# Hybrid block (Nystrom attention, FP4 feed-forward, linear attention): order of work where the first feed-forward meets linear attention

## The reference

```python
x = x + attn_a(layernorm(x), w_qkv, w_conv, w_fc, b_fc)
x = x + ffn(layernorm(x), w_gate, w_up, w_down)
x = x + attn_b(layernorm(x), W_attn, b_attn, W_proj, b_proj)
x = x + ffn(layernorm(x), w_gate, w_up, w_down)
```

```python
q, k = elu(q) + 1, elu(k) + 1          # the features
kv, ksum = kv + k_t v_t^T, ksum + k_t  # running sums over the tokens
y_t = (q_t kv) / (q_t . ksum + 1e-6)
out = y @ W_proj + b_proj
```

## Time and profile before

| | |
|---|---|
| median of 3 runs | 637.01 us (636.86 to 640.54) |
| the profiled execution | 637.31 us |
| its span, first to last instruction | 635.6 us |
| TensorE busy (matmul) | 577.8 us, 91% |
| VectorE busy | 487.4 us, 77% |
| ScalarE busy | 361.4 us, 57% |
| GpSimd busy | 303.3 us, 48% |
| mean granted clock of TensorE | 0.984 |

### The profile page before, as it was taken

How to read it: one execution, slowest core, us unless ns; L and a number is a source line. 1 busy time by engine, 2 the same in 40 slices (tenths; PEclk the granted TensorE clock), 3 DMA queues, 4 the chain that set the end, 5 groups by cost and what they waited for, 6 DMA issues and landing times.

```text
span 635.6 us, 14058 instructions
## 1 busy us (share of the span) xinstructions
PE 577.8 (91%) x5407; PEld 426.2 (67%) x5407; DVE 487.4 (77%) x1004; ACT 361.4 (57%) x679; POOL 303.3 (48%) x351
## 2 busy tenths in 40 slices
PE   4889998799999999987999988999999988599997
PEld 3777887466666679964777765656656655377776
DVE  6978888466666664887999876778778786889975
ACT  5643322344444443157998774556556557699975
POOL 6542111122223223546788677255554435667763
PEclk9999999799999999998999999999999999999999
DMA  9500000000000001000000000000000000000101
GB/s 248 135 2 1 3 2 2 1 1 1 2 1 2 1 3 35 2 0 1 1 2 2 1 1 1 3 2 2 2 2 2 1 3 2 1 18 18 34 18 51
DMA packets 15942, 9.58 MB, mean 15 GB/s; under 512 B 1478, under 2 KB 15750, under 8 KB 15876
## 3 DMA queue, kind: packets, MB, share of 16 engines
q1 hardware_dynamic: 15876, 8.69, 5.1%
HBM read 6.59 MB, written 2.10 MB: 14 GB/s over the span
## 4 chain that ended last, share of the span: by engine, by line
PE 43%; DVE 23%; POOL 14%; issue 11%; ACT 8%; DMA 1%; SPq 0%; POOLq 0%; DVEq 0%; ACTq 0%
PE ps L1440 6%; PE ps L1597 4%; PE ps L1456 4%; PE ps L1614 4%; PE ps L1635 3%; PE ps L1743 3%; PE ps L1619 3%; DVE r L965 3%; POOL G L335 3%; DVE m L1016 3%; PE ps L1447 3%; ACT S L549 2%; POOL arena L429 2%; ACT qbd L578 2%; PE ps L1630 2%
## 5 line engine op out<-in xcount | busy, mean ns | idle before, releaser
L394 POOL TENSOR_TENSOR A<-S,r 126x512 f32<-126x512 f32 x36 | 38.0, 1057 | 147.6 <-DVE r L968 132.9
L429 POOL TENSOR_SCALAR_AFFINE_SELECT arena<-arena 128x1024 f32<-128x1024 f32 x32 | 35.9, 1121 | 65.6 <-ACT arena L802 65.5
L1614 PE MATMUL ps<-wguT,xnt 128*128 128x352 f32 x128 | 52.1, 489 | 8.1 <-ACT xnt L642 5.4
L335 POOL TENSOR_TENSOR G<-S,hoff 128x704 f32<-128x704 f32 x31 | 47.1, 1520 | 24.9 <-DVE S L1112 24.7
L1635 PEld LDWEIGHTS ps<-wdT,xnt 128*128 128x128 f32 x372 | 48.5, 191 | 8.2 <-ACT xnt L649 1.4
L1635 PE MATMUL ps<-wdT,xnt 128*128 128x128 f32 x372 | 51.9, 275 | 0.9 <-ACT xnt L649 0.9
L802 ACT ACTIVATE arena<-ps 128x1024 f32<-128x1024 f32 x32 | 32.7, 1022 | 33.9 <-PE ps L1743 33.9
L1280 DVE TENSOR_TENSOR arena<-ps,XN 128x1024 f32<-128x1024 f32 x32 | 39.2, 1224 | 14.8 <-PE ps L1743 14.8
L965 DVE TENSOR_REDUCE r<-S 126x16 f32<-126x512 f32 x36 | 24.7, 685 | 33.4 <-ACT S L549 33.4
L1619 PE MATMUL ps<-wguT,xnt 128*128 128x352 f32 x128 | 44.2, 469 | 0.0
L549 ACT ACTIVATE S<-S 126x512 f32<-126x512 f32 x36 | 22.5, 625 | 38.1 <-DVE S L960 38.1
(11 more groups left out here) (225 smaller groups left out, 1520.2 us busy)
## 6 DMA issues: line engine op xcount, KB each, us to landing
X<-in_x SPq DMA_DIRECT2D x8, 256.0 KB, 5.5
out<-X SPq DMA_DIRECT2D x7, 256.0 KB, 2.3
arena<-in_wqkvT SPq DMA_DIRECT2D x4, 256.0 KB, 5.4
band<-in_band SPq DMA_DIRECT2D x1, 897.8 KB
arena<-in_wqkvT SPq DMA_DIRECT2D x1, 512.0 KB, 7.7
early<-in_wfc SPq DMA_DIRECT2D x1, 512.0 KB, 9.4
kI<-in_scaled_eye SPq DMA_DIRECT2D x1, 192.0 KB
XN<-in_wattn SPq DMA_DIRECT2D x1, 192.0 KB, 2.4
```

The lines of the kernel that those rows point to most:

```text
L335: tt(out=hgrid, in0=hmoved[k], in1=hoff[k][:, :], op=ALU.subtract).then_inc(s["fh_grid"], 1)
L394: tt(out=A1v[:, w % NW, :].rearrange("p (h m) -> p h m", m=M), in0=S1v[:, w % NW, :].rearrange("p (h m) -> p h m", m=M), in1=r1[:, 3, w % ...
L429: nc.gpsimd.affine_select(out=masked[n % 2][:, 8:16, :], in_=raw.rearrange("p (h t) -> p h t", t=P), pattern=[[0, 8], [1, P]], compare_op= ...
L1614: mm(ps[:, GATE_BANK, 0:F], xT[t // QD % 2][:, t % QD, :], wguT[:, 0:F], start=True, stop=True).then_inc(s["f_gate"], 1)
```

## The change

Seven edits in the hand-written orders:

- VectorE makes only h = 0 and 1 of the first quad's diagonals; ScalarE makes h = 3 and 2 in step r = 17 of the feed-forward, behind `lin_spread(0)` and `lin_xbT(1)` and ahead of `hT_copy(15)`. TensorE's wait in `lin_scores` counts ScalarE's two for every quad.
- TensorE issues `lin_k_mm(1)` directly behind `lin_scores(0)`, ahead of the last `down_mms`. ScalarE issues `lin_exp_k(1)` behind `lin_raw(0)`, ahead of the last `down_copy`.
- VectorE issues `lin_phi(1)` ahead of `lin_mask(1)`.
- GpSimd issues `lin_select(1)` and `lin_qk(1)` ahead of `layernorm_moments(2, 7)` and `lin_bias(1)`.
- VectorE issues `lin_v(0)` ahead of the statistics of step r = 16.
- ScalarE issues `down_copy(13)` between the two instructions of `offset_h(15)`.

```diff
--- before.py
+++ after.py
@@ -450,8 +450,6 @@
             lin_cap(1, eq, "lin_eq_done", "lin_eq_capped")
             lin_select(0)
             lin_cap(1, ek, "lin_ek_done", "lin_ek_capped")
-            layernorm_moments(2, QN - 1)
-            lin_bias(1)
             for n in range(TILES):
                 q, phase = (n + 1) // QD + 1, (n + 1) % QD
                 if n + 1 < TILES:
@@ -462,6 +460,9 @@
                         lin_cap(q, ek, "lin_ek_done", "lin_ek_capped")
                     if phase == 1:
                         lin_qk(q)
+                    if n == 0:
+                        layernorm_moments(2, QN - 1)
+                        lin_bias(1)
                     if phase == 2 and q + 1 < TILES // QD:
                         lin_bias(q + 1)
                 if n % QD == 1 and n > QD:
@@ -667,6 +668,8 @@
                     a.wait_ge(s["fh_ratio"], n + 1)
                     need(a, "fh_grid", n - 1)
                     act(hoff[r % 2][:, :].rearrange("p (k n) -> p k n", k=2), up_banks(r), ACT.Square, scale=SQ).then_inc(s["fh_offset"], 1)
+                    if p == 0 and r == PN - 1:
+                        down_copy(r - 2)
                     a.wait_ge(s["fh_offset"], 2 * n + 1)
                     act(hoff[r % 2][:, :], hoff[r % 2][:, :], ACT.Identity, bias=lnc[:, 3:4]).then_inc(s["fh_offset"], 1)
 
@@ -732,6 +735,8 @@
                     if p == 0 and r == PN + 1:
                         lin_spread(0)
                         lin_xbT(1)
+                        lin_qbd(0, 3)
+                        lin_qbd(0, 2)
                     if 0 <= r - 2 < PN:
                         hT_copy(r - 2)
                     if p == 0 and r == PN - 1:
@@ -753,7 +758,8 @@
                     if p == 0 and r == PN + 1:
                         lin_exp_q(1)
                         lin_raw(0)
-                    if 0 <= r - 2 < PN and (p == 0 or r < PN - 2):
+                        lin_exp_k(1)
+                    if 0 <= r - 2 < PN and (r != PN - 1 if p == 0 else r < PN - 2):
                         down_copy(r - 2)
                 return step, normalise, silu
             (step0, normalise0, _), (step1, normalise1, silu1) = ffn(0), ffn(1)
@@ -816,7 +822,6 @@
                     lin_norm(0)
                 if r == 14:
                     lin_xbT(0)
-            lin_exp_k(1)
             for n in range(TILES):
                 q, phase = (n + 1) // QD + 1, (n + 1) % QD
                 if n + 1 < TILES:
@@ -1217,6 +1222,8 @@
                         inverse("fh", hblk[r % 2], ffn_pairs(p, r))
                     if x_new:
                         ratio_x(q)
+                    if p == 0 and r == PN:
+                        lin_v(0)
                     if p == 0 and 0 <= r - 3 < PN:
                         v.wait_ge(s["f_x_done"], ffn_pairs(p, r - 2))
                         tile_stats(2, 2 * r - 6)
@@ -1270,7 +1277,7 @@
 
             def lin_qbd(q):
                 v.wait_ge(s["lin_qn_done"], q + 1)
-                for h in range(HR if q == 0 else HR // 2):
+                for h in range(HR // 2):
                     last = ts(out=qbd[q % 2][:, h, :], in0=qn[q % 2], scalar1=rowhead[:, h:h + 1], scalar2=None, op0=ALU.mult)
                 last.then_inc(s["lin_qbd_done"], 1)
 
@@ -1320,21 +1327,21 @@
                     v.wait_ge(s["lin_bias_qk"], 1)
                     lin_phi(0)
                     lin_scan(0)
-                if r == 16:
-                    lin_v(0)
             for n in range(TILES):
                 q, phase = (n + 1) // QD + 1, (n + 1) % QD
                 if n > 0:
                     lin_out(n - 1)
                 if q < TILES // QD and phase == 3:
                     lin_qn(q)
+                if n == 0:
+                    lin_phi(q)
                 if n + 1 < TILES:
                     lin_mask(n + 1)
                 if q < TILES // QD and phase == 3:
                     lin_qbd(q)
                 if n > 0:
                     lin_stats(n - 1)
-                if q < TILES // QD and (phase == 0 or n == 0):
+                if q < TILES // QD and phase == 0:
                     lin_phi(q)
                 if q < TILES // QD and phase == 1:
                     lin_scan(q)
@@ -1735,7 +1742,7 @@
             def lin_scores(n):
                 q, k = divmod(n, QD)
                 pe.wait_ge(s["lin_qbd_done"], q + 1)
-                need(pe, "lin_qbd_act", 2 * q)
+                pe.wait_ge(s["lin_qbd_act"], 2 * q + 2)
                 need(pe, "lin_masked_dve", n)
                 for r in range(RG):
                     if r == 2:
@@ -1802,7 +1809,7 @@
                     lin_q_mm(1)
                     pe.wait_ge(s["fh_moved"], ffn_pairs(0, PN))
                     lin_scores(0)
-            lin_k_mm(1)
+                    lin_k_mm(1)
             pe.wait_ge(s["f_x_done"], PN)
             for n in range(TILES):
                 q, phase = (n + 1) // QD + 1, (n + 1) % QD
```

## The result

| | before | after |
|---|---|---|
| median | 636.86 us (15 runs, 634.35 to 640.54) | 632.73 us (15 runs, 630.57 to 636.55) |
| the profiled execution | 637.31 us | 634.54 us |
| its span | 635.6 us | 632.8 us |
| mean granted clock of TensorE | 0.984 | 0.984 |

Run against run, after stands to before as 0.9941, with a 95% interval of 0.9922 to 0.996: 3.8 us faster, between 2.5 and 5.0. The forecast was 634.3 us (632.7 to 637.0), within 1%. The time is inside the range by 0.03 us, at its lower edge, and the gain is larger than forecast.

The account below looks back on a forecast made before the run. Bound: a chain hopping between engines from the first feed-forward into linear attention. 2.05 us up to second denominators plus 1.08 of clock, 3.1 off 637.31; weighed against the median too, 634.3 us (632.7 to 637.0).

Parts of the forecast that it names:

- Copy and v sum: End of the first feed-forward: ScalarE's copy and VectorE's v sum come earlier, so first denominators start 0.8 us sooner.
- S: Mark: the moment the first scores start on TensorE; 382.85 us before, forecast 381.5.
- Two diagonals on ScalarE: First quad's diagonals, split between ScalarE and VectorE, end by 381.4; with the front, S gains 1.35 us in all.
- Features ahead of the mask: Second quad on VectorE: features, then mask, then scan over at 391.05; with GpSimd's order, D gains 2.05 us.
- D: Mark: the start of the second denominators on TensorE; 394.46 us before, forecast 392.4.
- GpSimd's product ahead of the bias: Second quad: GpSimd's key-sum product starts at the scan's end, not 0.86 us after it.
- The clock: TensorE's stretch at 1.2 GHz behind D goes because its gap ahead of D shrinks; 1.08 us.
- (a): TensorE's clock falls at the first gap, scores lose about 0.45 us, second slow stretch stays: 635.6 us; chance 0.18.
- (b): Diagonals not done sooner, ScalarE's pair holds up copies, early key product eats the rest: 636.8 us; chance 0.13.
- (c): Features wait in front of the mask for a late key cap, TensorE idles: slower, 638.7 us; chance 0.06.
- the first rival: Experiments' theory: GpSimd's order carries the gain past first scores; reordering keys and features does nothing; no chance given.
- the clock rival: Experiments' theory: the clock decides, each edit counts only by the gaps it leaves on TensorE; no chance given.

Follow-up runs that it names:

- e5_front: Kernel after with ScalarE's copy back behind the offset and VectorE's v sum back behind the statistics; 634.42 us (1 run).
- h2_diag: Kernel after with all four first diagonals on VectorE, plus unread products in TensorE's waits ahead of the turn and first scores; 635.51 us (1 run).
- e2_key: Kernel after with key product, its exponential and the order of features and mask put back; 631.57 us (1 run).
- e3_phi: Kernel after with only the second quad's features put back behind the mask; 634.22 us (1 run).
- e1_diag: Kernel after with all four of the first quad's diagonals made by VectorE again; 635.69 us (1 run).
- g1_pool_only: Kernel before with one edit alone: GpSimd's second selection and key-sum product ahead of moments and bias; 632.87 us (1 run).
- e4_pool: Kernel after with only GpSimd's moments and bias put back ahead of the second selection and key-sum product; 633.82 us (1 run).
- f1_before_lin: Kernel before with seven unread products in TensorE's wait ahead of the second denominators; 635.64 us (10 runs), ratio to before 0.999.
- h3_before_fills: Kernel before with the unread products of f3_all; 632.42 us (12 runs), ratio to before 0.995.
- f3_all: Kernel after with unread products: 10 ahead of the first landmark transposes, 12 ahead of each feed-forward's first transposes; 626.72 us (6 runs), 0.9847 of before.
- h4_nokey: Kernel after with 10, 18, 18 and 2 unread products, and key product, exponential and features put back; 626.57 us (5 runs), 0.9873 of before.

## Why the prediction was right or wrong

- **What bounds the kernel.** Right. The chain through the same hops is the one on which all marks moved, and from the third quad on nothing changed (19.06 us per quad).
- **Copy and v sum, 0.8.** Right: 0.79 at the first denominators, given back by e5_front. Not all of it reaches the scores. h2_diag has the front edits and four diagonals on VectorE, and its S is 9.52, 0.56 before that of the kernel before: the chain comes 0.79 earlier, but then GpSimd's bias starts among the diagonals and not ahead of them, and the four take 2.69 us instead of 2.24.
- **Two diagonals on ScalarE, 0.55 beyond the front.** Mis-sized. The step that failed is the price of VectorE's pair: I took it near the 1.78 of a later quad's pair, because GpSimd's bias would run beside it, which gave S = 381.5. The two took 0.88 (VectorE had begun before the bias, and the bias waited), and ScalarE's pair (1.33) sets S: 8.25 from the scan, where the forecast's 1.35 of gain would give 8.73. Up to S the gain was 1.83 (0.56 and 1.27).
- **VectorE and GpSimd on one port.** The forecast weighed the Trainium skill, "SBUF — State Buffer", section "SBUF: two separate sides": who starts first holds the shared pair and the other waits. It took this to mean that VectorE waits for the bias, against its own times: VectorE at 379.67 was to begin ahead of the bias at 379.96. In after VectorE began at 379.90 and GpSimd's bias at 380.40, 0.38 us before VectorE's pair was through; the bias took 1.51 us instead of the 1.27 of the earlier trace rows. By that rule the trace agrees: who came first did not wait. It agrees for the four of before as well, in full and not in part: the first diagonal found the bias running, took 1.05 us and ended 0.28 behind the bias's end, and the other three took 0.47 each. The pair of 1.78 is one diagonal of 1.39 beside a selection and one of 0.47. So both prices that the forecast weighed were prices with a wait in them, and a diagonal without one (0.47) was in its own trace.
- **Key product behind the first scores, cost 0.6.** Right: second scores 0.54 later by e2_key, S + 4.45 where S + 4.5 was forecast.
- **Features ahead of the mask.** Right in the order and the lengths: counted from the scan, the features start at 13.50 without idle time in front of them (forecast 13.98) and the mask at 14.80 (forecast 15.38), earlier by about what S was earlier (0.48). Wrong as a source of gain: the forecast took D's gain past S from both this and GpSimd. The two edits cancel (e2_key, e3_phi).
- **GpSimd's product ahead of the bias, 0.86.** Right mechanism, too small. The product follows the scan at once, as worked out. What was missed is the scan itself: I took 1.76 us from the earlier trace rows as its own duration, and it was that of a scan that waits for GpSimd's bias, which ran from 389.92 to 391.19. Without that wait it takes 1.27 (after, e1_diag, g1_pool_only), and the edit puts the bias behind it. So the edit gives 1.25 (g1_pool_only) to 1.30 (e4_pool): 0.49 from the scan and the rest from the product. Gain up to D: 1.83 + 1.25 = 3.08, where 2.05 was forecast; of the 1.03 that the forecast lacks, 0.48 are the diagonals and 0.55 this.
- **What now waits behind the product.** Right: the third selection is over at 394.57 + 1.10 = 395.67, 22.54 from the scan where the forecast had 24.5, and TensorE did not wait for it (its third attend starts at 397.52 without idle time).
- **The clock, 1.08.** Right: 1.08 (20.14 - 19.06), seen in all kernels in which TensorE's gap ahead of D is shorter (0.44 to 0.72 us, where the forecast had 1.2), and in f1_before_lin, where only products without use were put in it. With a gap of 1.70 (before), 1.69 (h3_before_fills) or 2.01 (e4_pool) the slow stretch was there each time.
- **From the place to the whole.** The forecast carried 3.1 to the end, and 4.16 was gained in the place; of this the profiled execution shows 2.8, as its start was 0.36 later (the sum of what the slow stretches at 120 and 290 us and the start of both executions took) and 1.0 was lost at 550 us, in a stretch at 1.2 GHz. These vary from one execution to the next, and the forecast had no term for them but the range. The medians differ by 4.13 and the interval is 2.5 to 5.0 us, in which 4.16 lies. That the time is in the range is partly luck: the lower bound was set for one slow stretch more that goes, but the profiled execution of after has as low a mean clock as that of before (0.984). Instead two mis-sized terms gave 1.03 us more, and 0.03 us of the range were left.
- **The rivals.** (a), the clock falling at the first gap: not in after, but in e4_pool, which has the same program up to there, and it cost 0.82 at S where 0.45 was worked out. So it is an event with a chance, not a consequence of the order; of the four profiled executions with this program up to S (after, e2_key, e3_phi, e4_pool) one has it. (b) fell: VectorE did not wait, TensorE did not wait for the copies behind ScalarE's pair, and GpSimd's edit alone gives 2.35 with the clock. Only its key product held (0.54), and the features' place repays that. (c) did not occur: the key cap ended at 385.23 + 0.61 = 385.84, 12.71 from the scan (forecast 13.03), and VectorE was not idle ahead of the features.
- **Small sums.** Two of ScalarE's diagonals at 0.71 from 379.67 end at 381.09, not 381.15, and 1.6 off 637.31 in rival (a) is 635.7, not 635.6. Nothing hangs on either.

So the forecast's theory holds for front, diagonals and clock, with other sizes; the first rival is right from the first scores to D; the clock rival is right for 1.1 us here and for part of the spread, and what moves that part is the products of f3_all and h4_nokey, not the order.

## What to carry to other kernels

A duration read beside another engine's work is not the instruction's own: before it goes into a sum, look for the same instruction with the other engine idle, and look at what the other engine had begun just before it. On VectorE and GpSimd such a wait stands in the profile as a longer instruction and not as idle time. Where an edit moves one instruction earlier at a cost and another repays it, try the pair without both. And when medians spread by more than the edits under study, look at the granted clock behind every wait of TensorE of some microseconds: in this kernel 34 unread products there gave 0.5% alone and 0.9% on top of the new order (0.9847 against 0.9941), and the new order alone 0.6%.

## What the runs showed of the hardware that was not expected

- VectorE's scan (128x512, both inputs in SBUF) and GpSimd's work wait for each other, and the wait stands inside the duration. The first three lines are before's, at the second scan; the last two are before's at the third:

```profile
389.92 1.27 POOL L414 TENSOR_TENSOR X<-X,XN 128x512 f32<-128x512 f32 x1
390.51 1.76 DVE L1245 TENSOR_TENSOR_SCAN arena<-lnc,arena 128x512 f32<-128x512 f32 x1
391.14 2.02 POOL L429 TENSOR_SCALAR_AFFINE_SELECT arena<-arena 128x1024 f32<-128x1024 f32 x1
```

```profile
411.03 1.09 POOL L429 TENSOR_SCALAR_AFFINE_SELECT arena<-arena 128x1024 f32<-128x1024 f32 x1 [2.85 <-ACT arena L802]
...
411.43 1.76 DVE L1245 TENSOR_TENSOR_SCAN arena<-lnc,arena 128x512 f32<-128x512 f32 x1
```

At the third scan the selection began first and has its own 1.09 us; the scan ends 1.07 behind it. At the second the bias began first and has its own 1.27; the scan ends 1.08 behind it, and the selection, which began under the scan, 0.89 behind the scan. In each pair the one that began first is not slowed by the other, and the other ends some 0.2 us less than its own duration (1.27 and 1.09) behind it. That is what the rule of the section cited above says, and the trace agrees. The 3.72 us of VectorE's small instruction at 21 us, against 0.35 where it began first, are the same thing.
- A block diagonal on VectorE (128x512) takes 0.47 us when nothing disturbs it (0.88 for two, which overlap a little). One that finds GpSimd at work ends 0.28 to 0.29 behind GpSimd's instruction: 1.05 us in before, 1.49 and 1.50 in e1_diag and h2_diag, 1.39 in the later quads. In the later quads both start within 0.02 us of each other, and it is VectorE that waits.
- The granted clock behind the same gap is not the same in each execution of the same instructions: behind the first gap it did not fall in after, e2_key and e3_phi, and it was 0.50 from 376 to 378 in e4_pool.
- Twelve unread 128x128 products in a wait of 4.66 us left 2.00 us of it, and TensorE came out at 2.4 GHz: 2.29 us less up to the first down products than in after's execution.
